# Adjacency in one block, the top-k search over pairs of rows, and layer one's x-product made during the search

## The reference, cut to what matters

```
x_norm = xn / max(norm(xn over l), 1e-12)            # xn = x as (n, b, l)
mean_sim = einsum('nbl,mbl->nm', x_norm, x_norm) / B # 512 x 512
A = mean_sim where m is among the 153 nearest of n (not n itself), else 0
deg = A.sum(axis=0);  dinv = rsqrt(deg) where deg > 0, else 0
An = dinv[:, None] * A * dinv[None, :]
out = einsum('sd,sbl->dbl', An, einsum('nbl,lo->nbo', xn, adj)) + bias
```

## Time and profile before

| what | value |
| --- | --- |
| runs | 1780.71, 1784.02, 1786.39 us; median 1784.02 |
| profiled execution | 1781.9 us, its span 1779.8 us |
| mean granted TensorE clock | 0.931 |
| PE busy | 1557.4 us (88%) |
| DVE busy | 1286.9 us (72%) |
| ACT, POOL busy | 828.6 us (47%), 548.3 us (31%) |
| DMA | 106.14 MB in all |

### The profile page before, as it was taken

How to read it: one execution, slowest core, us unless ns; L and a number is a source line. 1 busy time by engine, 2 the same in 40 slices (tenths; PEclk the granted TensorE clock), 3 DMA queues, 4 the chain that set the end, 5 groups by cost and what they waited for, 6 DMA issues and landing times. The chain is left out here.

```text
span 1779.8 us, 27351 instructions
## 1 busy us (share of the span) xinstructions
PE 1557.4 (88%) x7776; PEld 1268.6 (71%) x7776; DVE 1286.9 (72%) x3046; ACT 828.6 (47%) x1381; POOL 548.3 (31%) x749
## 2 busy tenths in 40 slices
PE   7899470599999999999999999998599791799997
PEld 4678330478888888888888888876488691577775
DVE  5798799347766677666776667765477699599997
ACT  7775220134344443444434444343333591377775
POOL 5652020012123221232212322122100000599997
PEclk9999685799999999999999999999699895799998
DMA  5320200101001110011100111000442000244442
GB/s 210 106 72 1 94 0 0 47 25 42 24 30 47 47 41 23 30 47 47 41 22 31 47 47 41 18 12 25 171 143 95 0 0 0 71 144 146 145 143 106
DMA packets 57580, 106.14 MB, mean 60 GB/s; under 512 B 5888, under 2 KB 6016, under 8 KB 57536
## 3 DMA queue, kind: packets, MB, share of 16 engines
q1 hardware_dynamic: 57536, 105.60, 17.7%
HBM read 71.90 MB, written 33.69 MB: 59 GB/s over the span
## 5 line engine op out<-in xcount | busy, mean ns | idle before, releaser
L773 POOL TENSOR_TENSOR rs_a<-ve_a,neghalf 128x1 f32<-128x1 f32 x64 | 34.6, 541 | 495.4 <-DVE nm_a L767 495.4
L232 PE MATMUL acc<-xn_lo,xn_hi 128*128 128x512 f32 (+1 forms) x640 | 145.4, 358 | 5.0 <-DVE xn_lo L203 4.8
L198 ACT ACTIVATE xn_hi<-xn 128x512 fp32r<-128x512 f32 x128 | 80.6, 630 | 117.1 <-DVE xn L191 117.0
L232 PEld LDWEIGHTS acc<-xn_lo,xn_hi 128*128 128x128 f32 x640 | 102.3, 192 | 19.2 <-DVE xn_lo L203 10.4
L1566 PE MATMUL l_ps<-an_hi,xw_hi 128*128 128x512 f32 x256 | 105.5, 412 | 9.8 <-POOL xw_lo L1627 8.4
L223 PEld LDWEIGHTS acc<-xn_hi 128*128 128x128 f32 x512 | 95.6, 192 | 24.3 <-ACT xn_hi L198 7.7
L923 PE MATMUL l_ps<-an_hi,xw_hi 128*128 128x512 f32 x256 | 103.2, 403 | 6.5 <-DVE xw_lo L1263 6.3
L564 DVE MATCH_REPLACE8 work<-best,work 128x520 f32<-128x520 f32 x160 | 107.7, 685 | 0.0
L329 POOL TENSOR_TENSOR sq_lo<-sq,sq_hi 128x512 fp32r<-128x512 f32 x64 | 87.3, 1380 | 61.2 <-ACT sq_hi L296 61.0
L203 DVE TENSOR_TENSOR xn_lo<-xn,xn_hi 128x512 fp32r<-128x512 f32 x128 | 105.8, 827 | 0.4 <-ACT xn_hi L198 0.2
L923 PE MATMUL l_ps<-an_hi,xw_lo 128*128 128x512 f32 x256 | 101.3, 396 | 0.0
(11 more groups left out here) (239 smaller groups left out, 4869.5 us busy)
## 6 DMA issues: line engine op xcount, KB each, us to landing
xr<-in_x SPq DMA_DIRECT2D x32, 512.0 KB, 3.5
xin<-in_x SPq DMA_DIRECT2D x64, 256.0 KB, 2.6
between<-xo SPq DMA_DIRECT2D x64, 256.0 KB, 2.0
xres<-between SPq DMA_DIRECT2D x32, 512.0 KB, 3.7
xin<-between SPq DMA_DIRECT2D x64, 256.0 KB, 2.7
out<-xo SPq DMA_DIRECT2D x64, 256.0 KB, 2.0
raw_lang<-in_L_gnn_W_lang SPq DMA_DIRECT2D x1, 1024.0 KB, 5.5
raw_grav<-in_L_gnn_W_grav SPq DMA_DIRECT2D x1, 1024.0 KB, 7.9
```

The costliest lines, as they stand in the source:

```text
L198: self.nc.scalar.activation(self.hi[:, i % 4, :], self.xn[:, i % 4, :], ACT.Copy).then_inc(self.hi_ready, 1)
L232: mm = self.nc.tensor.matmul(out, h[:, c * P:(c + 1) * P], l[:, a:b], start=False, stop=False, skip_group_check=True)
```

## The change

- `whole_similarity`, `choose` and `normal_adjacency` become one block, `adjacency`, on eight PSUM banks that are held from the similarity sums on.
- Assembly: ACT and DVE copy hi*lo out without the factor; row 0 is added as before; for rows 1 to 3 PE adds the turned and the plain hi*lo onto the hi*hi banks with f32 products against the identity. The factor 1/64 goes into `deg` and `dcol`. The search of rows 0 and 1 starts when these stand; ACT finishes rows 2 and 3.
- Search: rows 0 and 1 in one loop of 19 rounds, then rows 2 and 3 in another. Each pair is followed by its `a`, now written into `sim`.
- Root: ACT square root (its table is loaded by a first call on `warm`) and DVE reciprocal in place of POOL's power. `an` is written into `work`; POOL makes an_lo of rows 0 and 1, DVE of rows 2 and 3.
- First instance: the last 32 batches of x stay in their ring from the similarity; PE makes x*adj for all 64 batches under the search, ACT copies them to an eight-deep `stage`, SP stores them to `xw_dram` (256 KB each) and loads the other 32 batches back, and the weights' sixteen jobs are put between batches 16 to 61.
- Layer pair: `xw(i)` is gone from PE. SP loads the product into a two-deep tile `xw`, ACT and DVE split it there. `l0` uses two banks by turns, which are also those of `hturn`.

The diff, cut to its core:

```diff
+            def largest(p):
+                pair = (2 * p, 2 * p + 1)
+                dve.sem_inc(marked[p], 2)
+                with dve.Fori(0, rounds) as r:
+                    for k, c in enumerate(pair):
+                        dve.wait_ge(marked[p], 2 * r + k + 1)
+                        own_step(dve, passed)
+                        nc.vector.max(best[:, c, :], work[:, c, :]).then_inc(found[p], 1)
+                    for k, c in enumerate(pair):
+                        dve.wait_ge(found[p], 2 * r + k + 1)
+                        own_step(dve, passed)
+                        mark(p, c)
...
+                dve.wait_ge(lower, CH - 1)
+                for k, c in enumerate(pair):
+                    dve.wait_ge(marked[p], 2 * (rounds + (1 if rest else 0)) + k + 1)
+                    nc.vector.scalar_tensor_tensor(out=sim[:, c, :], in0=row_of(c), scalar=CHOSEN, in1=sim[:, c, :],
+                                                   op0=ALU.is_equal, op1=ALU.mult).then_inc(chosen, 1)
...
+            nc.vector.tensor_copy(hl_sb[:, 3, :], at.hl[3]).then_inc(dve_hl, 1)
+            nc.vector.tensor_copy(hl_sb[:, 2, :], at.hl[2]).then_inc(dve_hl, 1)
...
+            nc.vector.tensor_tensor(sim[:, 0, :], g[:], part, ALU.add).then_inc(row0, 1)
...
+            mask(1)
+            dve.wait_ge(masked, 2)
+            largest(0)
+            dve.wait_ge(copied, 3)
+            mask(2)
+            mask(3)
+            dve.wait_ge(masked, 4)
+            largest(1)
...
+            pe.wait_ge(act_hl, 2)
+            pe.wait_ge(dve_hl, 2)
+            for j in range(CH):
+                mm = nc.tensor.transpose(g[:, j * P:(j + 1) * P], hl_sb[:, j, 0:P], s.ident[:])
+            mm.then_inc(t0_made, 1)
+            for j in range(1, CH):
+                add_turned(at.hh[1][:, (j - 1) * P:j * P], 1, j)
+            add_plain(at.hh[1][:, 0:P], hl_sb[:, 1, P:2 * P])
+            add_turned(at.hh[3], 3, 3)
+            add_plain(at.hh[3], hl_sb[:, 3, 3 * P:N]).then_inc(raised, 1)
...
+                for n, b in enumerate(order):
+                    sp.wait_ge(xw_out, n + 1)
+                    sp.dma_start(xw_dram[b], stage[:, n % 8, :]).then_inc(xw_stored[n % 8], 16)
+                    if n + RING < nb:
+                        sp.dma_start(xr[:, b % RING, :], x[order[n + RING]]).then_inc(x_back[n % 4], 16)
...
+                for n in range(nb):
+                    early_xw(n)
+                    if n in after:
+                        prepare(after[n])
...
+            act.wait_ge(warmed, 1)
+            nc.scalar.activation(warm[:], warm[:], ACT.Sqrt)
+            act.wait_ge(dve_done, 2)
+            nc.scalar.activation(root[:], deg[:], ACT.Sqrt).then_inc(rooted, 1)
...
+            for c in (0, 1):
+                pool.wait_ge(hi_ready, c + 1)
+                nc.gpsimd.tensor_tensor(s.an_lo[:, c, :], row_of(c), s.an_hi[:, c, :].bitcast(F32), ALU.subtract)
...
-        ht_ps = xw_ps, l0_ps = ps("xw_ps"), ps("l0_ps")
+        ht_ps = l0_ps = [ps("l0_ps0"), ps("l0_ps1")]
...
-                for kind, i in (("store", 0), ("store", 1), ("load", 0), ("store", 2), ("store", 3),
-                                ("load", 1), ("load", 2), ("load", 3)):
-                    if kind == "load" and ga is not None:
+                for kind, i in (("here", 2), ("here", 3), ("store", 0), ("store", 1), ("load", 0), ("next", 0),
+                                ("store", 2), ("store", 3), ("load", 1), ("load", 2), ("next", 1), ("load", 3)):
...
-                def xw(i):
-
-                    pe.wait_ge(x_loaded[i], 16 * (ga + 1))
...
-                    for c in range(CH):
-                        mm = nc.tensor.matmul(xw_ps[:, c * P:(c + 1) * P], xin[:, i, c * P:(c + 1) * P], s.adj[:],
-                                              start=True, stop=True)
...
-                    copy(xw_hi[:, i % 2, :], xw_ps[:]).then_inc(xw_hi_ok, 1)
+                    copy(xw_hi[:, i % 2, :], xw[:, i % 2, :]).then_inc(xw_hi_ok, 1)
...
-                    lo_part(xw_lo[:, i % 2, :], xw_ps[:], xw_hi[:, i % 2, :], xw_lo_ok)
+                    lo_part(xw_lo[:, i % 2, :], xw[:, i % 2, :], xw_hi[:, i % 2, :], xw_lo_ok)
```

More of the change, by code:

```diff
@@ L474, in _, with adjacency @@
                 sums.crosses(pe, i)
-def whole_similarity(nc, s, acc, sim, work):
+def adjacency(nc, s, banks, weights, xres, early):
     nb = s.nb
-    at = Layout(acc)
-    with ExitStack() as ctx:
[L482 to L491, removed]
-            for c in range(CH):
[L493 to L540, removed]
@@ L543, in choose @@
[L543 to L550, removed]
+    rounds, rest = TOP // 8, TOP % 8
+    at = Layout(banks[:6])
+    g, h = banks[6], banks[7]
+    turned = {1: (h, 0, P), 2: (banks[3], 0, 2 * P), 3: (banks[4], 0, 3 * P)}
+    xw_ps, prep = banks[:4], banks[4:6]
+    with ExitStack() as ctx:
+        sb, _, sem = scope(nc, ctx)
+        sim, work = sb("sim", [P, CH, N]), sb("work", [P, CH, 8 + N])
+        best, stage = sb("best", [P, CH, 8]), sb("stage", [P, 8, N])
+        hl_sb, part = stage[:, 0:CH, :], stage[:, CH, :]
+        diag = sb("diag", [P, CH, P])
+        deg, pos, root, dinv, dcol = (sb(n, [P, CH]) for n in ("deg", "pos", "root", "dinv", "dcol"))
+        warm = sb("warm", [P, 1])
+        row_of = lambda c: work[:, c, 8:8 + N]
+        act_hl, dve_hl, t0_made, parted, row0, raised = (
+            sem(x) for x in ("act_hl", "dve_hl", "t0_made", "parted", "row0", "raised"))
+        upper, low_made, lower, copied, masked, assembled = (
+            sem(x) for x in ("upper", "low_made", "lower", "copied", "masked", "assembled"))
+        found, marked, passed = [sem(f"found{p}") for p in range(2)], [sem(f"marked{p}") for p in range(2)], sem("passed")
+        chosen, summed, dve_done, rooted, spread, made_an, hi_ready = (
+            sem(x) for x in ("chosen", "deg_summed", "n_dve", "n_rooted", "spread", "made_an", "n_hi"))
+        warmed = sem("warmed")
@@ new lines, in _, with batch, bring, take @@
+            act.wait_ge(upper, 3)
+            act.sem_inc(assembled, 1)
+            for c in (2, 3):
+                copy(row_of(c), sim[:, c, :]).then_inc(copied, 1)
+            if weights is not None:
+                for n in range(nb):
+                    take_xw(n)
+                    if n in after:
+                        take_weights(after[n])
+            else:
+                def batch(b):
+                    return xres[:, bass.ds(b, 1), :].rearrange("p a n -> p (a n)")
+                def bring(b, k):
+                    copy(x_at[:, k, :], batch(b)).then_inc(x_there, 1)
+                def take(b, k):
+                    act.wait_ge(xw_made, b + 1)
+                    copy(batch(b), xw_ps[k][:])
+                for k in range(4):
+                    bring(k, k)
+                with act.Fori(0, nb // 4 - 1) as q:
+                    for k in range(4):
+                        take(4 * q + k, k)
+                        bring(4 * q + 4 + k, k)
+                for k in range(4):
+                    take(nb - 4 + k, k)
```

418 lines of the change are left out of this document (220 added, 198 removed).

## The result

| | before | after |
| --- | --- | --- |
| median of four runs, us | 1783.01 | 1727.14 (1725.8 to 1728.88) |
| profiled execution, its span, us | 1781.9, 1779.8 | 1727.61, 1725.8 |
| mean granted clock | 0.931 | 0.954 |

The ratio is 0.9686, with a 95% interval of 0.9667 to 0.9705. Forecast were 1728.5 us and a range of 1708 to 1748. The five runs of the same kernel beside the experiments gave 1727.7 us, ratio 0.9678 (0.9664 to 0.9691).

The account below looks back on a forecast made before the run. PE was taken to bound the layer turns, DVE's chain the adjacency. Two blocks at -8.75 (-17.5) and the layer's -38.0 made -55.5, from 1784.02 to 1728.5 us; range 1708 to 1748.

Parts of the forecast that it names:

- assembly: Before each block's search: search starts once rows 0 and 1 stand, 8.0 us for 14.03; -6.0 (4.5 to 7.8).
- search: Each block's search: two loops of 19 rounds at 2.54 us replace rounds of 5.08; +0.65 us (0 to +2).
- rounding: an_lo in each block: POOL makes two subtractions while DVE makes two; -0.5 us, bounds -1.0 and +0.3.
- steady turn: Full layer turn sheds four xw products: seam gives 0.37, two middle places 0.9 each; -2.17 us per turn.
- first turn to yprod(0): Layer's start: load split at once, shorter waits before l0(1), l0(2), -4.0 us (2 to 4.2); seam to turn 1, -0.9.
- layer pair: Whole layer: -30.4 for 14 turns, -4.0 start, -0.9 seam, -2.7 for three products in turn 1; -38.0 us.
- The slower rival, the back edge: Pair search's 76 loop edges: 0.2 us exposed per round gives 1743, fully exposed 1825; chance 0.07 in all.
- Under the search: First block's search hides products, copies, stores, loads and weights' work free; 25.2 MB over near 283, search near 304.
- The rival of a transfer bound at 210 GB/s: First search: 25.2 MB take 120 us, end at 324 and delay PE's column sums; +10 us, 1739; chance 0.06.
- The rival in which PE gets all it sheds: Layer turns: no seam chain holds PE back, 14 x 1.6 us more gained; 1706 us; chance 0.12.
- the rival of a turn that turns into waits: Layer turns: l0(2) or yprod(3) meets a late DVE, one us lost per turn; 1745 us; chance 0.13.
- its clock may rise later: Layer's first turns: PE starts later, so its clock may rise later; given within the bounds 2 and 4.2 of -4.0.

Follow-up runs that it names:

- experiment 1: The changed kernel, unaltered, measured again as the yardstick for the other runs: 1727.7 us.
- experiment 4: The changed kernel with the 19 search rounds of each pair written out instead of looped: 1726.88 us, ratio 0.9673.
- Experiment 6: The changed kernel with the inverse root by POOL's power instead of ACT's square root and DVE's reciprocal: 1731.01 us.
- experiment 7: The changed kernel with all four an_lo subtractions on DVE, none on POOL: 1725.71 us.
- experiment 3: The changed kernel with every xw stored a second time to another tensor, 16.8 MB more under the first search: 1735.0 us.
- experiment 9: The changed kernel with two xw-sized products that feed nothing, ahead of yprod(2) and yprod(3) in 15 layer turns: 1755.58 us, ratio 0.9836.
- experiment 10: The changed kernel with PE's hturn(3) ahead of both squares and ACT's next first split ahead of the sums: 1707.59 us, ratio 0.9568.
- Experiment 12: The changed kernel with f32 products that feed nothing wherever PE idles in the layer's first turn: 1722.65 us, ratio 0.9658.
- Experiment 11: The kernel of experiment 10, with all four xw of the first turn split ahead of residuals and statistics: 1699.61 us, ratio 0.9519.

## Why the prediction was right, point by point

The total is within 1.4 us of the forecast, and in part by luck: the fall was 54.0 us by the spans of the two profiles, for a forecast of 55.5, and terms erred against each other.

| term | forecast | measured by the two profiles |
| --- | --- | --- |
| assembly, per block | -6.0 (4.5 to 7.8) | -7.9 and -6.4 |
| search | +0.65 | +0.3 |
| column sums | -2.3 | -2.2 |
| root | -0.6 | -0.7 |
| rounding | -0.5 (-1.0 to +0.3) | 0.0 |
| both blocks | -17.5 | -18.7 |
| steady turn | -2.17 | -2.10 |
| first turn to yprod(0) | -4.0 and -0.9 | -3.5 |
| layer pair | -38.0 | -34.9 (+0.4 in the second similarity) |

The terms of the two blocks add up to -19.5. Of the 0.8 that come back, 0.2 lie between the row product and the first `an`, and 0.6 behind the last subtraction: the next part's first instruction follows it by 0.96 and 1.59 us in place of 0.82 and 1.16.

- **Assembly.** Right in both its prices: I gave 6.2 us at the high clock and 9.5 at the low one and took 8.0, with the clock falling in between. The second block did that (7.74 at 0.78), the first ran at full clock (6.13). That was chance: of the twelve profiles of kernels with pairs five have the first at 6.13, the others between 7.46 and 7.78. At the 7.77 us of experiment 1 the term would be -6.3.
- **Search.** The forecast's own terms add up to 105.7 us and not to the 105.9 written there, so to +0.45; measured are +0.3. The round of two keeps its rate, as said, and the entry of the second loop is 0.42 us and not up to 1.28. The slower rival, the back edge, falls with experiment 4: the rounds are as long with the edges as without. The Trainium skill (Runtime: NRT & Kernel Launch, "Instruction fetch mechanics") has a taken branch stall when its target lies outside the fetched pages. No such stall shows in the 76 edges; whether these bodies ever cross such a bound no run here shows.
- **Column sums and root** came as forecast. Experiment 6 gives the root back by 0.77 when the power returns.
- **Rounding** is the term that failed in its value, not in its bounds: I took the middle between no collision and the 1.44 of the earlier trace rows. POOL's two subtractions keep 1.27 us each and end at 313.06. DVE's first starts at 311.83, beside POOL's second, and lasts 1.78 in place of 0.68, to 0.55 after POOL's end; its second takes 0.68 again. So they run one after the other: 310.56 + 2.50 + 1.25 (half of 2.49) is 314.31, and DVE ends at 314.21. The Trainium skill (SBUF — State Buffer, "SBUF: two separate sides") calls the port pair that the two engines share an exclusive lock, held for a whole instruction. The trace agrees with it. The +0.3 that the forecast allowed for this case was too dear: in series the four cost what they cost on DVE alone (5.14 and 5.13 us, experiment 7).
- **Under the search.** Costless it was, but the forecast's measure, 25 MB at 334 GB/s until near 283, was the wrong one. The queues moved 397 GB/s as long as there was both to load and to store, and then idled at 149 GB/s from 250 on, since PE, which I had not counted, was busy without a break with products and weights' jobs. The last stores were issued at 290 to 292, and PE waited 9.1 us for the last rows. The margin is that of PE: 9 us, not 20. The rival of a transfer bound at 210 GB/s is excluded by experiment 3.
- **The steady turn.** The mechanism is shown. I gave 0.9 to each product in the middle, and experiment 9 has 1.79 for two. That leaves 0.31 of the 2.10 for the two at the seam, forecast at 0.37. The rival in which PE gets all it sheds falls: 1.57 us a turn were missing, and experiment 10 shows the chains at the seam to be the reason, since with their order changed the turn gives them. PE's idle before the turn of k is 0.31 us by its row, where near 0.7 was announced; 0.7 is the distance of the starts. Of the rival of a turn that turns into waits nothing shows: the steady turn has no wait but those of the seam.
- **Layer pair.** 3.1 us were missing: 1.0 by fourteen times 0.07, 2.1 in the first turns, forecast at 7.6 in all (4.0, 0.9 and 2.7) and measured at 5.5 (3.5 to yprod(0), 2.0 in turn 1, 52.36 to 50.32, if the turn behind it is counted at its steady length; from one yprod(0) to the next turn 1 alone falls by 1.3, 52.18 to 50.89). The step that failed is "its clock may rise later", which widened a bound and was priced at nothing. By its parts: start -1.85 (forecast -2.1), ahead of l0(1) -1.5 (-1.0), of l0(2) -0.9 (-1.0), of l0(3) 0 (0), from hturn(2) to yprod(0) -0.9 (-0.9). But l0(3) at 1.2 GHz costs +1.6, and in turn 1 ten instructions run at that level where three did before, +1.4 at 0.2 each. The products that were taken out had also kept PE at work between l0(0) and l0(3). Experiment 12 shows that idle of PE is the cause: with useless products in it no instruction of l0(3) or of turn 1's beginning is at the low level. Experiment 11 parts the two. With the waits between the l0 gone and no product added, l0(3) keeps the high level, so it fell there for the waits of 1.53, 1.49 and 2.79 us. Turn 1 still begins at the low level, so its low instructions must come from the idle behind l0(3). As the rows read, the cold xw at the head of turn 1 before (2.07 us from 361.15) had taken most of that low stretch on itself; taken out, it leaves it to yprod(0) and l0(0).

## What to carry to other kernels

Work taken off the busiest engine pays in full only where nothing else is late at that spot: read each place by itself, and where a chain of other engines ends there, rearrange it along with the work (here one turning on PE ahead of the squares and one split on ACT ahead of `sums`, 20 us together). Before hiding work under a stage, add up every engine that does it, not only the queues. And work that is removed from PE between waits can cost by the clock what it saves by its length.

## What was not expected of the hardware

- Loads and stores of 256 KB together ran at 374 to 403 GB/s for 100 us, from 210 to 310 (experiment 3), where the only stretch of loads alone in the earlier trace rows showed 334, and DVE's search beside them kept its 2.54 us a round.
- 47 useless f32 products made a stretch of 138 us 6.2 us shorter.
- The same assembly of 28 matmuls takes 6.13 or about 7.7 us, by the clock that PE happens to have; two executions of one program differ in it (first block, 6.13 in the one profile, 7.77 in the other).
- A DVE subtraction of two SBUF tiles that met one of POOL's took 1.78 us in place of 0.68, and POOL's kept its 1.27; sharing the work between them gained nothing (5.14 and 5.13 us).
